# Units 2 and 3 of a cross-interaction kernel: three of four Bs by DMA and ScalarE instead of by TensorE

## The reference

```python
e = stack([tbl_f[ids[:, f]] for f in range(24)], axis=1)       # X0: 1024 x 24 x 16
Xk = e
for W in (W0, W1, W2):                                         # 64 outputs each
    Wr = W.reshape(24, Xk.shape[1], 64)
    Xk = einsum('bfd,bhd,fho->bod', e, Xk, Wr)                 # X1, X2, X3
    outs.append(Xk.sum(axis=2))
h = concatenate(outs + [dense_ctx], axis=1)
h = maximum(h @ W_top1 + b_top1, 0); h = maximum(h @ W_top2 + b_top2, 0)
y = h @ W_top3
```

## Time and profile before

| | us |
|---|---|
| median of 3 runs | 378.74 |
| lowest and highest of them | 377.19, 379.49 |
| the profiled execution | 375.55 |
| its span, first to last instruction | 373.7 |

### The profile page before, as it was taken

The page is one execution under the profiler, slowest core; times in us unless marked ns, Lnnn a source line. Parts: engine busy times, 40 slices in busy tenths (PEclk is TensorE's granted clock), DMA queues, the critical chain, the costliest instruction groups (busy, mean ns, idle before and its releaser), DMA issues.

```text
span 373.7 us, 7214 instructions
## 1 busy us (share of the span) xinstructions
PE 353.9 (95%) x2754; PEld 160.2 (43%) x2754; DVE 307.8 (82%) x308; ACT 187.4 (50%) x352; POOL 220.0 (59%) x332
## 2 busy tenths in 40 slices
PE   0958999999999999999999999999999999999997
PEld 0736623322333345434343454444443444444475
DVE  2993399969897999979898999798999999997600
ACT  1112024146352667574747475837474676545564
POOL 5888888888887878888863888888840000000000
PEclk9978999999999999999999999999999999999999
DMA  7686998979989799989999799979996999540000
GB/s 205 217 160 147 230 165 193 231 166 214 232 196 247 149 232 257 247 178 226 237 241 247 171 254 264 256 147 248 270 251 139 239 257 257 145 139 0 3 2 2
DMA packets 56773, 71.55 MB, mean 191 GB/s; under 512 B 31041, under 2 KB 35777, under 8 KB 56738
## 3 DMA queue, kind: packets, MB, share of 16 engines
q1 hardware_dynamic: 49282, 69.56, 77.8%
q0 software_dynamic: 5376, 1.39, 3.6%
q10 hardware_dynamic: 2080, 0.13, 0.4%
HBM read 50.61 MB, written 1.58 MB: 140 GB/s over the span
## 4 chain that ended last, share of the span: by engine, by line
PE 88%; DVE 7%; ACT 2%; DMA 1%; issue 1%; SPq 0%; DVEq 0%; ACTq 0%
PE ps_x L436 55%; PE ps_b L436 10%; PE ps_tower L436 10%; PE ps_turn L436 7%; DVE Z L373 4%; PE ps_turn L492 3%; PE ps_tower L442 2%; PE ps_turn L500 2%; DMA small_ids_sb<-small_ids 1%; DVE Z L412 1%; ACT x_diag L729 1%; DVE small_ids_f L368 1%; DVE Z L402 1%; DVE x_diag L381 0%; ACT C L702 0%
## 5 line engine op out<-in xcount | busy, mean ns | idle before, releaser
L412 DVE TENSOR_TENSOR Z<-A,ps_b 128x1024 f32<-128x1024 f32 x192 | 221.0, 1213 | 9.8 <-PE ps_x L436 5.5
L230 POOL DMA_INDIRECT x_rows<-tbl,ids_sb x168 | 179.4, 1068 | 55.1 <-POOL pause_sb L241 30.6
L436 PE MATMUL ps_x<-Z,w_sb 128*64 128x512 f32 x768 | 184.2, 598 | 0.7 <-DVE Z L412 0.5
L436 PEld LDWEIGHTS ps_x<-Z,w_sb 128*64 128x64 f32 x768 | 49.3, 136 | 79.9 <-issue 56.1
L402 DVE TENSOR_TENSOR Z<-A,C 128x1024 f32<-128x1024 f32 x48 | 57.6, 1220 | 25.2 <-PE ps_x L436 8.8
L729 ACT ACTIVATE x_diag<-ps_turn,mask_sb 128x192 f32<-128x192 f32 x128 | 50.6, 607 | 14.6 <-PE ps_turn L500 14.6
L436 PE MATMUL ps_x<-Z,w0s_sb 128*64 128x512 f32 x192 | 45.2, 597 | 0.5 <-DVE Z L402 0.3
L241 POOL MEMSET pause_sb<- 128x144 f32 x160 | 40.4, 252 | 0.1
L712 ACT COPY ps_b<-B_sb 128x1024 f32<-128x1024 f32 x36 | 36.9, 1025 | 4.4 <-DMA B_sb<-x_sb 4.0
L742 ACT COPY G<-ps_turn 128x416 f32<-128x416 f32 x31 | 15.7, 505 | 46.7 <-PE ps_turn L436 45.6
L436 PEld LDWEIGHTS ps_turn<-x_diag,x_rows 128*64 128x64 f32 x496 | 25.2, 137 | 17.7 <-issue 17.7
(11 more groups left out here) (60 smaller groups left out, 184.9 us busy)
## 6 DMA issues: line engine op xcount, KB each, us to landing
A<-x_scratch SPq DMA_DIRECT2D x48, 512.0 KB, 11.9
B_sb<-x_sb SPq DMA_DIRECT2D x72, 256.0 KB
C<-x_scratch SPq DMA_DIRECT2D x32, 512.0 KB, 13.2
x_rows<-tbl,ids_sb POOLq DMA_INDIRECT x168
small_ids_sb<-small_ids SPq DMA_DIRECT2D x3, 512.0 KB, 6.1
x_quarters<-x_scratch SPq DMA_DIRECT2D x16, 96.0 KB
x_scratch<-x_rows SPq DMA_DIRECT2D x7, 192.0 KB
w_sb<-w SPq DMA_DIRECT2D x2, 384.0 KB, 5.2
```

The source lines that it names most:

```text
L230: pool.indirect_dma_start(out=x0_rows[t % 2][:, f * D:(f + 1) * D], out_offset=None, in_=tables[f], in_offset=bass.IndirectOffsetOnAxis(ap ...
L412: nc.vector.tensor_tensor(Z[s % ZR][:, :], A[u % AS][i][:, :], ps_b[j % 2][:, :], ALU.mult)\
L436: return nc.tensor.matmul(out, lhsT, rhs, start=start, stop=stop)
```

## The change

PB becomes 2. Units 2 and 3 now take only B 0 from TensorE; their B 1 to B 3 are spread by twelve DMAs and copied to PSUM by six copies of ScalarE, as in the units from 4 on. The counts that the engines wait for (made_b, and the waits on b_in and b_copied) follow from PB.

```diff
 FIRST = (6, 6)
 
-PB = 4
+PB = 2
 PER_SLOT = NI + NP2
```

## The result

| | before | change |
|---|---|---|
| median, us | 378.98 | 384.93 |
| lowest and highest of 4 runs | 377.19, 379.49 | 382.35, 386.89 |
| profiled execution, its span | 375.55, 373.7 | 384.59, 382.8 |

The change is slower: ratio 1.0181, 95% interval 1.0129 to 1.0233, 5.95 us on the medians (4.9 to 8.8 us by the interval). Some 1.4 us of this arise before the changed stretch begins (the turn of X2 in step 1 stands at 69.52 instead of 68.13), so 7.7 us of the 9.1 between the spans are the change's in this execution.

What follows compares the result with a forecast made beforehand. TensorE, at 95% busy, was taken as the bound beside full DMA engines whose loads barely keep ahead. Profiled 375.55 us plus 4.7 for late loads is 380.25, plus 3.2 to the median 383.4; range 377.5 to 387.0.

Steps and rivals of the forecast that it cites:

- the sum: Whole run: the largest lateness, 4.7 us in unit 9's step, reaches the end as loss; own range 1.7 to 7.3.
- TensorE and VectorE, 4.8 us less 0.9: Units 2 and 3: fewer TensorE Bs save 4.8 us, a VectorE wait costs 0.9; 3.9 us ahead at unit 4.
- The wait for the C copies: VectorE's third product of X1 near 89 us waits 0.9 us, because B 1 of unit 2 is copied first.
- SP, moved: SP's queue: B loads ahead of tile 2's store push it and unit 4's loads some 3 us later; costed at nothing.
- the stall at 89: VectorE's wait for the C copies near 89 us, put at 0.9; to be judged worse if unit 5 began at 128 or later.
- DMA, added: Twelve transfers, 3.15 MB: 11.3 us less 5.3 idle makes loads from unit 6 on 6.0 us late (3.0 to 8.6).
- The price of 11.3 us: DMA time of the twelve added transfers, 3.15 MB at 278 GB/s; bounds 10.3 and 12.7 us.
- The rival of a faster way: SBUF-to-SBUF Bs fit into 7.3 us of idle time at 431 GB/s, so loads aren't late: 378.3 us; chance 0.08.
- What covers it: Later steps: full DMA engines give nothing back until 205 us; the lead leaves units 7, 9, 13 late by 3.5, 4.7, 4.0.
- the lead of 2.5, 1.3 and 0.4 us: Time to spare between B 1's landing and TensorE's turn of X2 in the steps of units 7, 9 and 13.
- The 1.6 us that were to come back before unit 13: Half of the 3.2 us of free DMA time from 281 to 288 us, assumed to recover 1.6 us.
- The signs: Expected in the trace: unit 5's X1 near 124.5, unit 6's loads near 133.7, B 1 waits, unit 9's copy near 230.5.

Runs made afterwards that it cites:

- e2_idle_bytes: Kernel before plus the change's twelve transfers into a buffer nobody reads, TensorE still making all Bs; 386.2 us, ratio 1.0248.
- e3_small_loads: The change with its twelve transfers cut to 64 of 512 columns, so Bs of units 2 and 3 are incomplete; 376.17 us, ratio 0.9952 to the kernel before.
- e5_c_first: The change with ScalarE's C copies put ahead of its copy of B 1; 384.21 us, ratio 1.0182 to the kernel before.
- e8_store_first: The change with SP issuing the next tile's store ahead of the B loads from unit 5 on; 380.17 us, ratio 1.0055 to the kernel before.
- e1_pb3: The change with PB 3, so unit 2 stays as before and six transfers are added; 379.8 us, ratio 1.0038 to the kernel before.
- e9_weights_later: The change with the tower's weights issued one unit later; 388.28 us, ratio 1.0305 to the kernel before.

## Why the prediction was right

**The direction and its cause hold.** Bytes in full DMA engines take more than TensorE saves: e2_idle_bytes and e3_small_loads separate the two. By medians the loss is 5.95 us, the sum said 4.7 (1.7 to 7.3); the interval of the measured loss, 4.9 to 8.8, begins just above it. That the two came so near is in part luck: the delay was taken too small, and the stall at unit 4 that the sum lacks only took the 3.9 us which it let be spent later (e2_idle_bytes, which never had them, is 7.4 us late at step 13 with its start taken off, the change 7.7).

**TensorE and VectorE, 4.8 us less 0.9.** Right in size: e3_small_loads is 3.8 us ahead at step 4, the working said 3.9. The wait for the C copies was 1.06 us, forecast 0.9. In the change itself these 3.9 never appear.

**SP, moved: wrong.** "Unit 4's loads are needed after 105, and I put this at nothing by itself." VectorE waited 4.1 us for A of unit 4. Its C loads were issued at 95.86 instead of 89.71: 1.4 of the 6.2 from the start of this execution, the rest from the Bs ahead of them. In e3_small_loads, with the same issues and an eighth of the bytes, they were issued at 91.28. The cover that I took for wide was smaller than that, and the loss begins a tile sooner than I said. So X1 of unit 5 began at 132.24, not near 124.5, and by the prediction's own words ("at 128 or later, the stall at 89 was worse") something was worse; it was not the stall at 89, as e5_c_first shows, but the one at 106 to 113.

**DMA, added: right in kind, the idle time too large.** The row gave 4.1 us free, and I took 5.3. The shares after show 3.0 used: 0.57 x 2 + 0.11 x 4 + 0.69 x 2; in e2_idle_bytes, which begins when before did, it is 3.4. 11.3 - 3.0 = 8.3 instead of 6.0. C of unit 6 was issued 8.5 us later (136.23, before 127.72), or 7.1 without the 1.4 at the start. The price of 11.3 us, at 278 GB/s, wasn't contradicted: the window of e2_idle_bytes gives 11.8. The rival of a faster way wanted 431 GB/s, and where these transfers were nearly alone they ran at 240 with a share of 0.90, so it fell. "305 at best" holds for the rows that the prediction shows, not for the trace: from 90 to 92 us, where the tower's weights and the loads of unit 4 move and no B, the kernel before reached 369. The Trainium skill, page DMA: Bandwidth & Descriptors, section Where 436 GB/s comes from, has transfers inside SBUF bound by the fabric at 435; the Bs stayed far below it here, at 240.

**What covers it: right in shape, not in its reason.** The forecast let the change be 3.5 us late at step 7, 4.7 at step 9 and 4.0 at step 13. Without the 1.4 of the start it was 5.2, 6.6 and 7.7. With the lead of 2.5, 1.3 and 0.4 us added back, that is 7.7, 7.9 and 8.1: one delay of about 8 us, eaten into by the lead as counted. e3_small_loads says the same: at steps 7, 9 and 11 the change is 8.1, 8.1 and 7.9 us behind it. The 1.6 us that were to come back before unit 13 didn't. And "the engines are full between the stores" was not the whole reason why nothing is given back before: e8_store_first moves the same bytes, and between its C loads of units 6 and 12 lie 116.3 us (132.18 to 248.44), where before had 118.9 and the change 120.6.

What the 4.7 left out is that SP's order feeds a delay back: B of unit 4 was issued 5.4 us later, which took the 5.1 us that SP had stood ahead of the store, and the store then landed behind those bytes, 11.1 instead of 5.3 us from store to load. The runs with the store first add nothing after step 5, while the change, e1_pb3, e3_small_loads, e5_c_first and e9_weights_later, with the old order, lose 2.6 to 3.9 us each against before from step 5 to step 13. So the growth of the loss hangs on the order. One trace doesn't fit in full: e2_idle_bytes, with the old order, stops losing at step 7. What part of the delay of unit 6's loads is bytes and what part the waits of SP for ScalarE, no run tells apart.

**The signs.** Late loads of unit 6, B 1 copies that wait in the steps of units 5, 7 and 9, TensorE idle before the turn: all seen. X1 of unit 5 near 124.5 was not. Unit 9's B 1 came at 233.76, or 232.4 without the 1.4, where 230.5 was said.

## What to carry to other kernels

Before work goes from a busy engine to DMA, look past the engines' shares to the stretch that is changed: if its DMA share is near one, added bytes can cost more time than the engine saves, and here the next loads in the queue paid first, not those some units on. Count free time only as the windows show it, and check how late the nearest consumer's data lands, with its number, before its delay is put at nothing. In an in-order queue see what stands behind each transfer: a store that must land before loads can start should not stand behind transfers that wait for another engine.

## What was unexpected of the hardware

After the waits at X1 of unit 4 TensorE's granted clock fell: 0.90 in the window of 106 to 123, where before it was 1.00, so part of the stretch ran at 1.2 instead of 2.4 GHz. Twelve MATMULs took 4.10 us at 117.58 where they took 2.80, 1.3 us more on TensorE behind waits of VectorE. In e2_idle_bytes the same window has 0.80, in e8_store_first 1.00, which may be a part of why its early steps lie nearer to before.

The issue of the load behind a store, one DMA on SP's queue, took 1.7 to 5.6 us for tiles 3 to 7 of before and 6.4 to 8.2 in the change; with the Bs between store and load it took 0.9 to 1.1 (e8_store_first). The store right behind six B transfers is not needed for a long issue: in e1_pb3, where SP had stood 5 us ahead of the store, it took up to 7.8. Of the gathers, the pause of 144 columns was worth 0.6% of the kernel before.
